# One ViT layer with post-LN and a top-2 expert MLP in fp32: routing weights from a tanh on ScalarE, two LN1 tiles scaled on ScalarE, and TensorE's order changed between the experts' first products

## The reference

```python
h = einsum(patchify(x), W) + b                      # 576 x 192
q, k, v = split(h @ w_qkv.T)                        # 12 heads of 64
q = q * rsqrt(norm(q, over heads) + 1e-8)           # the same for k
att = softmax(q @ k.T / scale) @ v @ w_out.T + b_out
h = layernorm(h + att)                              # LN1
logits = h @ Wr + br                                # 8 experts
vals, idx = top_k(logits, 2);  share = softmax(vals)
gu = minimum(h @ Wgu[e] + bgu[e], 7)                # for each expert e
a = (maximum(up, -7) + 1) * gate * sigmoid(1.702 * gate)
h = layernorm(h + sum_j share_j * (a @ Wd[idx_j] + bd[idx_j]))   # LN2
```

## Time and profile before

| | |
|---|---|
| median of 3 runs | 139.73 us (139.38 to 139.88) |
| the profiled execution: time | 139.37 us |
| the profiled execution: span, first to last instruction | 137.6 us |
| PE busy | 128.9 us (94%) |
| DVE, ACT, POOL busy | 97.4, 78.7, 77.3 us |
| mean granted TensorE clock | 0.994 of full speed |

### The profile page before, as it was taken

How to read it: one execution, slowest core, us unless ns; L and a number is a source line. 1 busy time by engine, 2 the same in 40 slices (tenths; PEclk the granted TensorE clock), 3 DMA queues, 4 the chain that set the end, 5 groups by cost and what they waited for, 6 DMA issues and landing times. The chain is left out here.

```text
span 137.6 us, 3992 instructions
## 1 busy us (share of the span) xinstructions
PE 128.9 (94%) x1564; PEld 119.8 (87%) x1565; DVE 97.4 (71%) x267; ACT 78.7 (57%) x152; POOL 77.3 (56%) x89
## 2 busy tenths in 40 slices
PE   6999899999999999999999999986999999999960
PEld 2779899999889889999989989976999998998950
DVE  0019489837868959447778886898888774788853
ACT  3048589989854458488768631541445445333761
POOL 7302238961278998998752664689934332344600
PEclk9999999999999999999999999999999999999997
DMA  4999954630022222522490068400001655000022
GB/s 128 325 401 406 405 183 138 210 133 0 9 76 53 67 67 57 159 62 80 151 323 27 0 144 198 102 0 0 0 0 37 155 140 122 2 5 0 2 59 70
DMA packets 8987, 15.47 MB, mean 112 GB/s; under 512 B 1224, under 2 KB 5896, under 8 KB 8968
## 3 DMA queue, kind: packets, MB, share of 16 engines
q1 hardware_dynamic: 8968, 15.22, 35.3%
HBM read 9.96 MB, written 0.44 MB: 76 GB/s over the span
## 5 line engine op out<-in xcount | busy, mean ns | idle before, releaser
L523 POOL TENSOR_TENSOR reg_r<-reg_p,reg_r 128x324 fp32r<-128x324 f32 (+1 forms) x23 | 18.6, 810 | 20.5 <-ACT reg_r L759 20.4
L457 POOL TENSOR_TENSOR reg_w<-stage,reg_w 128x768 fp32r<-128x768 f32 x12 | 22.3, 1871 | 7.8 <-ACT reg_w L587 5.4
L759 ACT ACTIVATE reg_r<-reg_p 128x324 fp32r<-128x324 f32 (+1 forms) x23 | 10.2, 444 | 13.7 <-DVE reg_p L1142 13.5
L1344 PE MATMUL ps<-reg_r,reg_w 128*128 128x324 f32 (+1 forms) x48 | 15.1, 315 | 2.2 <-DVE reg_p L1142 2.2
L750 ACT ACTIVATE ps<-ps,sm 128x252 f32<-128x252 f32 (+1 forms) x21 | 9.7, 464 | 11.1 <-PE ps L1348 10.8
L1345 PE MATMUL ps<-reg_r,reg_w 128*128 128x324 f32 (+1 forms) x48 | 14.2, 295 | 0.0
L1347 PE MATMUL ps<-reg_r,reg_w 128*128 128x324 f32 (+1 forms) x48 | 14.2, 295 | 0.0
L1346 PE MATMUL ps<-reg_r,reg_w 128*128 128x324 f32 (+1 forms) x48 | 14.2, 295 | 0.0
L1348 PE MATMUL ps<-reg_r,reg_w 128*128 128x324 f32 (+1 forms) x48 | 14.2, 295 | 0.0
L1107 DVE TENSOR_SCALAR ps<-ps,bup 128x252 f32<-128x252 f32 (+1 forms) x21 | 10.7, 510 | 3.1 <-PE ps L1348 3.0
L493 POOL TENSOR_TENSOR reg_q<-reg_q,rnorm 128x432 f32<-128x432 f32 x7 | 8.9, 1275 | 6.4 <-ACT rnorm L665 6.4
(11 more groups left out here) (207 smaller groups left out, 393.3 us busy)
## 6 DMA issues: line engine op xcount, KB each, us to landing
reg_x<-xw_in SPq DMA_DIRECT2D x5, 416.0 KB, 6.0
stage<-w_gu_a SPq DMA_DIRECT2D x4, 384.0 KB, 4.0
stage<-w_gu_b SPq DMA_DIRECT2D x4, 384.0 KB, 3.4
reg_r<-reg_x SPq DMA_DIRECT2D x24, 54.0 KB
stage<-w_qkv_a SPq DMA_DIRECT2D x3, 384.0 KB, 7.8
stage<-w_qkv_b SPq DMA_DIRECT2D x3, 384.0 KB, 8.1
stage<-w_down SPq DMA_DIRECT2D x3, 384.0 KB, 3.7
stage<-wrow SPq DMA_DIRECT2D x8, 126.0 KB, 2.4
```

The lines of the kernel that those rows point to most:

```text
L457: nc.gpsimd.tensor_tensor(dst[:, 1, :], raw, f(dst[:, 0, :]), ALU.subtract).then_inc(s_wlop, 1)
L523: nc.gpsimd.tensor_tensor(acts[:, n % NACT, 1, 0:w], act_f[:, n % 4, 0:w], f(acts[:, n % NACT, 0, 0:w]), ALU.subtract).then_inc(s_alo, 1)
L759: nc.scalar.activation(acts[:, n % NACT, 0, 0:w], act_f[:, n % 4, 0:w], ACT.Copy).then_inc(s_ahi, 1)
L1344: mm(out_ap, w_a(0), x[:, 0, cols], start=True, stop=False)
```

## The change

The change has four parts, all between LN1 and the last routing weights.

- Routing. `gap_exp` on POOL and `router_weights` on DVE (five small instructions a tile) are gone. `shares(b)` on ACT takes their place: one tanh of half the gap, a copy of the two indices to float, and two scaled copies, for tiles 0 to 2 together and for tiles 3 and 4 each.
- LN1 of tiles 3 and 4. The two scaling instructions move from DVE to ACT (`ln1(g)` there), and DVE makes the bias, -mean * rstd, in one instruction on a column (`ln1_bias`).
- Tile 3 is transposed into columns 324 to 447 of banks 5 and 6 (`ACC`, beside the sums of the first half) and no more into bank 4, and its logits go to bank 5.
- Order. On PE, `gate_up(3)` and `spread(1)` come ahead of the third tile's transposes, `project(4)` follows these, `residual(0)` moves behind `gate_up(4)`, and `logits(3)`, `h1_transpose(4)`, `logits(4)` and `w_transpose(1)` stand earlier. DVE, ACT and POOL are ordered to match.

```diff
@@ PE
             gate_up(2)
             spread(0)
-            residual(0)
-            h1_transpose(3)
             gate_up(3)
             spread(1)
+            h1_transpose(3)
             project(4)
             spread(2)
+            logits(3)
+            gate_up(4)
+            residual(0)
+            h1_transpose(4)
             down(0)
-            gate_up(4)
             down(1)
-            logits(3)
             gate_up(5)
             down(2)
-            h1_transpose(4)
+            logits(4)
             gate_up(6)
             down(3)
             gate_up(7)
-            logits(4)
+            down(4)
             gate_up(8)
-            down(4)
+            down(5)
+            w_transpose(1)
             gate_up(9)
-            down(5)
             down(6)
@@ PE, project(g) and residual(0)
-                if g == 4:
-                    pe.wait_ge(s_h1lo, 8)
+                    pe.wait_ge(s_h1lo, 8)
+                    pe.wait_ge(s_lg, 4)
@@ ACT
+            def ln1(g):
+
+                n = TSIZES[g]
+                act.wait_ge(s_nb, g - 2)
+                act.wait_ge(s_ht, g - 1)
+                for src, dst in ((slice(0, D), slice(0, D)), (slice(DA, D), slice(D, D + DB))):
+                    nc.scalar.activation(h1[0:n, g % 2, dst], ps[0:n, L_BANK, src], ACT.Identity, bias=nbias[0:n, :],
+                                         scale=rstd[0:n, :]).then_inc(s_h1, 1)
+
+            def shares(b):
+
+                g0, g1 = CHOICES[b][0], CHOICES[b][-1] + 1
+                n = TSIZES[g0]
+                act.wait_ge(s_gap, g1)
+                nc.scalar.activation(th[0:n, g0:g1], gap[0:n, g0:g1], ACT.Tanh, scale=-0.5).then_inc(s_th, 1)
+                act.wait_ge(s_ti, g1)
+                nc.scalar.activation(index[0:n, g0:g1, :], top_i[0:n, g0:g1, 0:2], ACT.Copy).then_inc(s_idx, 1)
+                act.wait_ge(s_th, b + 1)
+                for j in range(2):
+                    nc.scalar.activation(share[0:n, j, g0:g1], th[0:n, g0:g1], ACT.Copy, scale=0.5 - j, bias=0.5)\
+                        .then_inc(s_share, 1)
@@ DVE
+            def ln1_bias(g):
+
+                n = TSIZES[g]
+                dve.wait_ge(s_rstd, g + 1)
+                nc.vector.tensor_scalar(nbias[0:n, :], mv[0:n, 0:1], rstd[0:n, 0:1], -1.0, ALU.mult, ALU.mult)\
+                    .then_inc(s_nb, 1)
...
-            def router_weights(g):
                 n = TSIZES[g]
-                rg = rt[:, g % 2]
-                dve.wait_ge(s_egap, g + 1)
-                nc.vector.tensor_scalar(rg[0:n, 6:7], rg[0:n, 3:4], 1.0, None, ALU.add).then_inc(s_rs, 1)
-                dve.wait_ge(s_rs, g + 1)
-                nc.vector.reciprocal(rg[0:n, 4:5], rg[0:n, 6:7]).then_inc(s_p1, 1)
```

More of the change, by code:

```diff
@@ L153, in vit_layer @@
         top = sb("top", [128, 8])
-        top_i = sb("top_i", [128, 2, 8], u32)
-        rt = sb("rt", [128, 2, 8])
+        top_i = sb("top_i", [128, NTT, 8], u32)
+        gap = sb("gap", [128, NTT])
+        th = sb("th", [128, NTT])
+        share = sb("share", [128, 2, NTT])
+        index = sb("index", [128, NTT, 2])
+        nbias = sb("nbias", [128, 1])
         w2 = sb("w2", [128, 3, 128])
@@ L209, in vit_layer, with choice_of @@
         W_BATCH = [(0, 1, 2), (3, 4)]
+        CHOICES = [(0, 1, 2), (3,), (4,)]
+        def choice_of(g):
+            return [b for b in range(3) if g in CHOICES[b]][0]
         s_x = [sem(f"s_x{i}") for i in range(NC)]
@@ L311, in lg_col, with turned @@
         def lg_col(g):
-            return LG_COL - 32 * (g == 3)
+            return LG_COL
         def lg_bank(g):
-            return B_BANK if g == 3 else ht_bank(g)
-        def ht_bank(g):
-            return (0, 2, 1, L_BANK, L_BANK)[g]
+            return (0, 2, 1, ACC, L_BANK)[g]
+        def turned(g):
+            n = TSIZES[g]
+            if g == 3:
+                return ps[:, ACC:ACC + 2, TS[0]:TS[0] + n]
+            return ps[:, lg_bank(g), HT_COL:HT_COL + 2 * n].rearrange("p (k n) -> p k n", k=2)
         def wt_bank(b):
@@ L411, in _ @@
             nc.gpsimd.memset(filler, 0.0).then_inc(s_filler, 1)
-            for t, value in ((ident[:, :], 0.0), (fold[:, :], 0.0), (half[:, :], -0.5), (euler[:, :], math.e),
+            for t, value in ((ident[:, :], 0.0), (fold[:, :], 0.0), (half[:, :], -0.5),
                              (w2[:, :, :], 0.0), (Pr2[:, :], 0.0)):
                 nc.gpsimd.memset(t, value).then_inc(s_fill, 1)
-            pool.wait_ge(s_fill, 6)
+            pool.wait_ge(s_fill, 5)
             def fill(ap, base, pattern, value, n):
@@ L562, in _ @@
             act_lo(7)
-            gap_exp(4)
             for n in range(8, LAST_LO):
@@ L727, in h1_evac @@
                 act.wait_ge(s_ht, g + 1)
[L728 to L730 removed]
+                nc.scalar.activation(h1T[:, 0:2, o:o + n], turned(g), ACT.Copy).then_inc(s_h1hi, 1)
+            def ln1(g):
[16 more added lines that the diff above has]
+                        .then_inc(s_share, 1)
             def w_rows(b):
@@ L817, in _ @@
             w_hi(14)
+            shares(0)
             o_evac(7)
@@ L825, in _ @@
             expert(2)
+            ln1(3)
+            expert(3)
             h1_evac(3)
-            expert(3)
             act_hi(0)
             act_hi(1)
+            expert(4)
+            ln1(4)
             act_hi(2)
-            expert(4)
+            h1_evac(4)
             act_hi(3)
+            shares(1)
             expert(5)
-            h1_evac(4)
             act_hi(4)
@@ L837, in _ @@
             act_hi(5)
+            shares(2)
             expert(7)
@@ L1235, in _ @@
             rank(1)
-            router_weights(0)
+            rank(2)
+            up_in(0)
             choose(0)
-            rank(2)
-            router_weights(1)
             choose(1)
-            router_weights(2)
             choose(2)
-            up_in(0)
             up_in(1)
@@ L1246, in _ @@
             w2_lo(0)
-            ln1(3)
+            ln1_bias(3)
             up_in(2)
@@ L1250, in _ @@
             expert_act(0)
+            up_in(3)
             h1_lo(3)
@@ L1253, in _ @@
             expert_act(1)
-            up_in(3)
+            ln1_stats(4)
+            read_logits(3)
             weigh(2)
+            ln1_bias(4)
+            expert_act(2)
             copy_iota()
-            expert_act(2)
             weigh(3)
             expert_act(3)
-            ln1_stats(4)
-            up_in(4)
-            ln1(4)
-            read_logits(3)
             rank(3)
-            weigh(4)
-            expert_act(4)
+            h1_lo(4)
+            expert_in(4)
+            choose(3)
             expert_in(5)
-            h1_lo(4)
-            router_weights(3)
-            choose(3)
-            expert_in(6)
-            expert_in(7)
             read_logits(4)
             rank(4)
+            expert_in(6)
+            choose(4)
+            expert_in(7)
             expert_in(8)
-            router_weights(4)
-            choose(4)
             for n in range(9, 2 * NT):
@@ L1708, in _ @@
                     down(n - 4)
-                if n == 10:
-                    w_transpose(1)
             for n in range(2 * NT - 6, 2 * NT):
```

54 lines of the change are left out of this document (17 added, 37 removed).

## The result

The changed kernel takes 137.93 us (median of 17 executions), the kernel before 139.63 us (17 executions, beside them on the same chip). The ratio is 0.9875, with a 95% interval of 0.9849 to 0.9901: faster by 1.2%, or 1.7 us. The forecast was 137.6 us with a range of 137.1 to 138.9.

The account below looks back on a forecast made before the run. PE was taken to bound the kernel, busy 128.9 of 137.6 us, so only its stalls could be won. Removing 2.22 us and adding 0.13 gave 2.09, from 139.73 to 137.6 us, range 137.1 to 138.9.

Parts of the forecast that it names:

- A: PE's stall ahead of `project(4)`, waiting for tile 3's low part in the shared bank: 0.13 us, forecast to go.
- B: PE's stall at `gate_up(6)` between transposes and its second product, released by `expert_act`: 0.73 us, forecast to go.
- C: PE's stall at `gate_up(8)` between logits and its second product, released by `expert_act`: 1.36 us, forecast to go.
- Tiles 0 to 2: Their routing leaves DVE ahead of `w_transpose(0)`, where it had stalled nothing on PE: no gain booked.
- the wait at the transposes: New PE wait at tile 4's transposes for LN1's scaled tile from ACT: 0.13 us, between none and 0.33.
- DVE's stretch to `expert_act(6)`: DVE's work from tile 4's statistics to `expert_act(6)`: 11.17 us, done at 94.90, 0.15 before PE reaches `gate_up(8)`.
- the waits that I had thought might vanish: 0.4 us of waits inside DVE's stretch, 0.19 and 0.21 of it printed, cited against the rival of DVE's lateness.
- The sum: 2.22 us of stalls removed less 0.13 of new wait: 2.09 us gained, 139.73 to 137.6.
- DVE comes late once or twice: Rival: DVE's lateness at `gate_up(8)` and `gate_up(9)` costs 0.5 to 1.3 us, giving 138.1 to 138.9; chance 0.22.
- The stalls change place: Rival: tile 3's low part delays `weigh(1)`, losing time at `spread(2)` and `gate_up(8)`: 139.2 to 139.7 us; chance 0.09.
- the table switch: Rival: tanh makes ACT reload tables in each of three `shares` calls, 5.4 us lost, 143.0; chance 0.03.
- One sign of being wrong: Named beforehand: PE's waits name `expert_act` again between 94 and 98 us.

Follow-up runs that it names:

- e8: The kernel before with only the routing arithmetic moved to ACT, old order kept; a repeat of e4 with more executions: 138.94 us, ratio 0.9942.
- e2: The changed kernel with LN1 scaling of tiles 3 and 4 put back on DVE: 137.66 us, ratio 0.9872.
- e7: The changed kernel with four more small, unused tanh instructions on ACT behind each call of `shares`: 137.70 us, ratio 0.9881.
- e4: The kernel before with only the routing arithmetic moved to ACT, old order kept: 141.37 us, ratio 1.0138.
- e3: The changed kernel with POOL's `act_lo(1)` made to wait until `expert_act(2)` on DVE is done: 137.24 us, ratio 0.9845.
- e9: The changed kernel with five one-column memsets added at the start of DVE's program: 138.95 us in one execution.
- e1: The changed kernel with only the routing arithmetic put back on DVE and POOL: 139.34 us, ratio 0.9999.
- e10: The kernel before with routing and LN1 scaling of tiles 3 and 4 moved to ACT, old order kept: 138.30 us, ratio 0.9926.
- e5: e3 with a second POOL wait, holding part of `w_lo(13)` until `expert_act(0)` is done: 137.46 us, ratio 0.9889 to the kernel before.
- e6: The changed kernel with LN1 scaling back on DVE and both POOL waits of e5: 137.29 us, ratio 0.9889.

## Why the prediction held, and where it was off

- **What bounds, and where the time is.** Right. PE's work is the same, A is gone, B is 0.14 instead of 0.73, C 0.29 instead of 1.36.
- **Routing.** Right in kind; neither it nor the order pays alone. With it and the old order 0.83 of the stretch is gained, with the new order and LN1 on ACT but without it 0.31, with all 1.62, more than their sum (1.14). The order is worth as much on top: with routing on ACT and LN1 on DVE, the old order has 26.16 (e8) and the new one 25.02 (e2). My reading, which no run tests by itself, is that the new order moves PE's demand, and only a relieved DVE meets it. A call of `shares` was 0.5 and not 0.8, without effect (e7).
- **Tiles 0 to 2.** Booked at nothing, and ahead of `spread(0)` worth nothing, 8.16 us from `gate_up(0)` to it in both. The prediction gave A's end to the new bank alone; e8 and e4 lose A with only the routing moved, so there the bank was not needed.
- **LN1 of tiles 3 and 4.** The price of the pair was right (0.9, measured 0.81), and the wait at the transposes (0.13, measured 0.10). That DVE loses 0.65 a tile was right as a sum of instructions and wrong as a gain: e2 shows that the move brings nothing, since the freed DVE runs into POOL (0.52) and into the pause (0.36), and e2 has neither.
- **DVE's stretch to `expert_act(6)`.** This is the term that was mis-sized. It was to last 11.17 and be 0.15 ahead of PE; it lasted 83.58 to 95.23, 11.65, and PE waited 0.29. In it are 0.52 from POOL over `expert_act(2)` (shown by e3) and 0.36 from the pause before `expert_act(3)` (e9 shows that it hangs on the place), 0.4 less elsewhere. That 0.4 is not the waits that I had thought might vanish: the printed 0.21 was already in the 0.81 that I took off, and counting it again was a mistake. What was shorter: reading and ranking tile 3 took 0.75 and not 0.87, `weigh(2)` 0.46 to the next instruction and not 0.59, `up_in(4)` 0.65 and not 0.75, bias and copy 0.21 and not 0.30. `gate_up(6)`, forecast as free, waited 0.14, and `gate_up(7)` 0.07; with e3's one wait on POOL the stretch is within 0.09 of the chart without a stall.
- **The sum.** 2.09 forecast, 1.62 measured in the stretch. The difference is the 0.50 at `gate_up(6)` to `gate_up(8)`, less the 0.03 that the transposes waited less. The spans differ by 1.8 because 0.21 came ahead of the stretch, where nothing had been forecast: that much of the agreement is luck. The rival "DVE comes late once or twice" came true in kind, at 0.5, the low end of its 0.5 to 1.3, though the time stayed within the forecast's 137.2 to 138.1; I had named slower single instructions for it, and not the other engine.
- **The stalls change place; the table switch.** Neither is seen. `spread(2)` and `project(4)` stand without a gap (81.00 to 83.53 is 2.53, and the prices give 0.22 + 2.19 + 0.15 = 2.56). ACT loads no table for tanh, which runs at 0.19.
- **The signs.** One sign of being wrong appeared, in small: PE's waits name `expert_act` before `gate_up(8)`, at 95.28. The idle time ahead of `gate_up(6)` and `gate_up(8)` is not none, and `gate_up(12)` came 1.83 earlier, not 2.1. The end behind it is the same, 31.3 us in both.

## What to carry to other kernels

Where one engine bounds, sum the starts of its rows against known prices, find the few stalls, and then add up the feeding engine's work to each deadline; a reorder pays only as far as the feeder keeps it, so small column work belongs on an engine with cover. When work leaves the feeder, look at what then runs beside its next instructions: here 0.65 us of freed time was used up by a POOL instruction that had been harmless and by a pause at a fixed place. A slack of 0.15 us on a sum of thirty instructions is none.

## What the runs showed of the hardware

**POOL holds up a DVE instruction that has two operands in SBUF.** `expert_act(0)` to `(2)` read gate and up both from SBUF, the later ones read one of them from PSUM. Under a POOL instruction the first kind took up to 1.03 instead of 0.50, by how much of POOL's was still to run; the second kind took 0.50 in e3 at 88.38, although POOL worked from 87.58 to 89.31. In the changed kernel `expert_act(2)` ended at 86.18, 0.35 behind POOL's end (85.83): it looks held until POOL let go. The same holds in each of twelve such meetings in the traces of the kernel before, the changed one, e1, e2, e3, e8, e9 and e10: the DVE instruction ends 0.34 to 0.36 behind POOL's end, with lengths from 0.52 to 1.03. The kernel before has one of them, `expert_act(0)` with 0.57 (81.06 to 81.63, POOL to 81.28). The Trainium skill, page "SBUF — State Buffer", section "SBUF: two separate sides", has this rule: DVE with two SBUF inputs and a GpSimd instruction that reads SBUF share a pair of ports, the first takes it for its whole duration, and the other waits. The trace agrees: 1.02 beside 0.50 for the same instruction, and 0.50 when POOL's is moved (e3, e5). The prediction did not use it.

**A pause at a fixed place in DVE's program.** About 0.36 us, before `expert_act(3)` in the changed kernel, in e3 and in e5, and three instructions earlier when five were put at the start (e9); it is not at this place in e1, e2 and e6. What it is was not shown.

**TensorE's clock drops in some executions.** In e4 it was 0.88 in the window from 68.5 us, 0.50 (1.2 GHz) in the next and 0.93 in the third; in the windows ahead of the fall and around it PE was busy 2.41 to 2.50 of 2.50 us, as in the changed kernel's trace, where the clock stayed at 1.00. e8's executions at 0.978 and 0.98 took 140.4, those at 0.954 took 142.9 to 143.2, the others 137.8 to 139.0. In the traces of e3, e5, e9 and e10 the clock fell too, between 69.9 and 71.5 us, and was full again before `spread(0)`, so the stretches can be compared.

The fall is not equally frequent in all kernels here. A mean clock of 0.985 or less had 19 of the 70 executions with `shares` on ACT, and 2 of the 51 without (the kernel before beside the experiments, and e1). So "the routing on ACT makes the fall likelier" is a rival that stays open; against it, e2 and e7 have `shares` too and had no fall in ten executions. It matters for the time: e8's mean over all twelve executions, 139.65, is that of the kernel before beside it, 139.65. In e5 and e6 two of six executions each were at 0.981 to 0.985 and are in their ratios; the others took 137.4 to 137.5 and 136.9 to 137.3.
